# Attention weights as a product of two exponentials and the adjacency, in a graph kernel with eight slots per loop body

## The chip, the cores and the metric

The kernel runs on one core of a Trainium2 chip. The metric is the device time of one execution in microseconds, as a median of several runs. The core's engines run side by side and meet only at semaphores: TensorE (PE in the profile, its weight loads PEld), VectorE (DVE), ScalarE (ACT), GpSimd (POOL) and SyncE (SP, which here only issues DMAs).

## The reference, cut to what matters

There are 64 graphs of 128 nodes with 128 features each; `adj` is a weighted adjacency matrix per graph. Two layers follow each other, each added to its input and normalised over the features.

```python
# layer 0, for each graph
hi = x @ W1[:H]; hj = x @ W1[H:]
h = relu(hi[:, None, :] + hj[None, :, :] + b1)      # 128 x 128 pairs of nodes, 128 features
y = layernorm(h @ W2 + b2) * gamma + beta
x = layernorm(x + einsum('ij,ijh->ih', adj, y))
# layer 1, for each graph
Wh = x @ W_w.T + W_b
si = Wh @ a_w[:C]; sj = Wh @ a_w[C:]
e = exp(si[:, None] + sj[None, :] + a_b) * adj
x = layernorm(x + (e / sum(e, axis=1)) @ x)
```

Nearly all arithmetic is in layer 0: 64 x 16384 pairs, each times a 128 x 128 matrix. The change lies in the two lines of layer 1 with `exp` and with the division by the row sum.

## The kernel before

A slot is one pass of the schedule over one graph. In slot t, four graphs are in work at different stages: the pair product of graph t ("pairs"), the preparation of graph t+1 ("prep": transposes of x and adj, products with W1), the weighted sum over the pairs of graph t-1 ("gather"), and all the rest of graph t-2 ("tail": back to the feature basis, first layernorm, attention, second layernorm, output). There are 66 slots, 0 to 65. The first 6 and the last 4 are written out; the 56 between are 7 turns of a loop whose body holds 8 slots.

A slot has 16 units. In each unit:

- GpSimd adds hi and hj for a block of 1024 columns (L259), four units ahead, in a ring of four buffers; it waits until TensorE has read the old block.
- ScalarE applies relu in place (L288), two units ahead, and then copies two quarters of the product, y, from PSUM to SBUF (L270). A quarter is one PSUM bank of four 128x128 tiles. Quarters are numbered through the slot, so unit u has quarters 2u and 2u+1.
- TensorE multiplies the relu's output by w_pair (L529), four 128x128 tiles into each of four rotating PSUM banks. Before a quarter it waits until VectorE has done with the quarter four before (q_done).
- VectorE multiplies y in PSUM by its copy in SBUF and sums along the row, one tile at a time (L515), four tiles a quarter, for the variance of the pair layernorm. It waits for the copy of each quarter.

Every TensorE product of 128x128 goes through `mm` (L529): four matmuls on the four groups of 32 columns of the array. In the trace each of these matmuls is two instructions (the data are float32), so one mm call shows as 8 matmul instructions. The weighted sums (L574, 8 instructions of 512 columns) follow the pair product in units 4, 6, 7, 9, 10, 12, 13 and 15.

Between these, in an order written out by hand by unit (u) and, on VectorE, by quarter of a unit (e), stand the small steps of the tail. VectorE has four such places e in each unit, and after each place it does two tiles of squares. The steps around the change, all on graph t-2:

- Unit 7: VectorE normalises into x1e (L469; x1e has a 129th column of ones, for the row sum), then forms the scores si (L472) and sj (L475), each one column.
- Unit 8: ScalarE spreads si over 128 columns, si_cols (L346).
- Unit 10: TensorE transposes si_cols into PSUM (L596); ScalarE takes exp with sj as bias (L351), which gives exp(s_i + s_j) with j on the partitions; VectorE multiplies by adjS, the adjacency transposed, into eT (L485).
- Unit 12: TensorE multiplies eT with x1e (L600): the weighted sum over the neighbours, and in column 128 the row sum. VectorE takes the reciprocal of the row sum (L488), scales and adds x1e (L492), and begins the statistics of the second layernorm (L496, L501).
- Unit 14: ScalarE forms the reciprocal root (L355, L357), VectorE writes x_out (L507), and SyncE stores it.

Two other steps stand near: in unit 9 TensorE makes the W1 products of the next graph and VectorE copies them out in `project`, at (9, 0); in unit 5 GpSimd copies adjT to adjS, behind a wait for the last reader of the old adjS.

Of the kernel before, what the change touches and what calls it, by code (L numbers as in the profile page):

```python
# [33 lines left out]
def gnn_pair_kernel(nc, x, adj, W1, b1, W2, b2, gamma, beta, Ww, Wb, aw, ab, out):  # L34
    F32 = mybir.dt.float32
    ALU = mybir.AluOpType
    ACT = mybir.ActivationFunctionType

    B, S, H = x.shape
# [23 lines left out]
    with ctx:  # L63
# [6 lines left out]
        def sem(name):  # L70
# [26 lines left out]
        sj, si, si_cols, s_terms = sb("sj", [S, 1]), sb("si", [S, 1]), sb("si_cols", [S, S]), sb("s_terms", [S, 2, K])  # L97
# [16 lines left out]
        eT = sb("eT", [S, S])  # L114
# [10 lines left out]
        x1p = ex = att_ps[:, 2 * K:3 * K]  # L125
# [17 lines left out]
        x1_ready, score_ps_s = sem("x1_ready"), sem("scores_in_psum")  # L143
        ex_ready, eT_ready, att_done = sem("exp_ready"), sem("eT_ready"), sem("attention_in_psum")
        rz_ready, x2p_ready, st2_ready, mv2_ready, ln2_ready, rs2_ready = sem("rz_ready"), sem("x2p_ready"), sem("st2_ready"), sem("mv2_ready"), sem("ln2_ready"), sem("rs2_ready")
        adj_sum_ready, beta_part_ready, x_beta_ready, sj_ready, si_ready, si_cols_ready = (
            sem(n) for n in ("adj_sum_ready", "beta_part_ready", "x_beta_ready", "sj_ready", "si_ready", "si_cols_ready"))
# [57 lines left out]
        def _(pool):  # L205
# [11 lines left out]
            def pair_weights(t, p, early):  # L217
# [8 lines left out]
                if early >= 3:  # L226

                    pool.wait_ge(eT_ready, t - 2)
# [39 lines left out]
        def _(act):  # L268
# [37 lines left out]
            def slot(t, half, p, pairs, prep, gather, tail, early):  # L306
                for u in range(UNITS):
# [36 lines left out]
                    if tail and u == 8:  # L344
                        act.wait_ge(si_ready, t - 1)
                        nc.scalar.activation(si_cols[:], ones[:], ACT.Identity, scale=si[:, 0:1]).then_inc(si_cols_ready, 1)  # L346
                    if tail and u == 10:
                        act.wait_ge(score_ps_s, t - 1)

                        act.wait_ge(sj_ready, t - 1)  # L350
                        nc.scalar.activation(ex, tail_ps[:, 3, :], ACT.Exp, bias=sj[:, 0:1]).then_inc(ex_ready, 1)  # L351
# [23 lines left out]
        def _(dve):  # L375
# [49 lines left out]
            def slot(t, half, p, pairs, prep, gather, tail, early):  # L425

                for u, e in ((u, e) for u in range(UNITS) for e in range(2 * QPU)):
# [43 lines left out]
                    if tail and (u, e) == (7, 1):  # L471
                        nc.vector.tensor_tensor_reduce(out=s_terms[:, 1, :], in0=x1p, in1=v1row[:], scale=rs1[:, 0:1], scalar=0.0,  # L472
                                                       op0=ALU.mult, op1=ALU.add, accum_out=si[:, 0:1]).then_inc(si_ready, 1)
                    if tail and (u, e) == (7, 2):
                        nc.vector.tensor_tensor_reduce(out=s_terms[:, 0, :], in0=x1p, in1=v2row[:], scale=rs1[:, 0:1], scalar=score_c[:, 0:1],  # L475
                                                       op0=ALU.mult, op1=ALU.add, accum_out=sj[:, 0:1]).then_inc(sj_ready, 1)
# [5 lines left out]
                    if tail and (u, e) == (10, 0):  # L482
                        dve.wait_ge(ex_ready, t - 1)
                        dve.wait_ge(adjS_ready, t - 1)
                        nc.vector.tensor_tensor(eT[:], ex, adjS[:, p, :], ALU.mult).then_inc(eT_ready, 1)  # L485
                    if tail and (u, e) == (12, 0):
                        dve.wait_ge(att_done, t - 1)
                        nc.vector.reciprocal(rz[:], att_ps[:, K:K + 1]).then_inc(rz_ready, 1)  # L488
                    if tail and (u, e) == (12, 1):
# [4 lines left out]
                    if tail and (u, e) == (12, 2):  # L494
                        dve.wait_ge(x2p_ready, t - 1)
                        nc.vector.bn_stats(st2[:], x2p).then_inc(st2_ready, 1)  # L496
                    if tail and (u, e) == (12, 3):
# [27 lines left out]
        def _(pe):  # L525
# [52 lines left out]
            def slot(t, half, p, pairs, prep, gather, tail, early):  # L578
                for u in range(UNITS):
# [13 lines left out]
                    if tail and u == 10:  # L593

                        pe.wait_ge(si_cols_ready, t - 1)
                        mm(tail_ps[:, 3, :], si_cols[:], ident[:]).then_inc(score_ps_s, 1)  # L596
                    if tail and u == 12:
                        pe.wait_ge(eT_ready, t - 1)
                        pe.wait_ge(x1_ready, t - 1)
                        mm(att_ps[:, 0:K + 1], eT[:], x1e[:]).then_inc(att_done, 1)  # L600
# [44 lines left out]
```

## Time and profile before

| | |
|---|---|
| median of 3 runs | 2457.67 us (2455.99 to 2457.86) |
| the profiled execution | 2456.72 us |
| its span, first to last instruction | 2454.9 us |
| granted TensorE clock, mean | 0.994 of full speed |
| busy, share of the span: TensorE matmul | 2390.1 us, 97% |
| ScalarE | 2231.9 us, 91% |
| VectorE | 2117.0 us, 86% |
| GpSimd | 2022.4 us, 82% |
| DMA read and written over the span | 9 GB/s |

The busy times of an engine's instructions overlap in the trace, and on TensorE strongly: a matmul's record is longer than its distance to the next. The page's chain of waits follows the work that ended last back from the last instruction; its shares are PE 83%, ACT 9%, "issue" 4%, DVE 3%. "issue" is time in which the engine waited for nothing that the profile shows.

### The profile page before, as it was taken

What the parts mean: (1) busy time and instruction counts of PE and PEld (TensorE: products, weight loads), DVE (VectorE), ACT (ScalarE), POOL (GpSimd) and SP (SyncE); (2) the same over time, 40 slices, a digit from 0 to 9 for tenths busy, and PEclk for the clock granted to TensorE, in tenths of its full rate; (3) what the DMA queues carried; (4) which work ended last, traced back from release to release, by engine and by line L of the source; (5) the groups of instructions that cost most, each with busy time, mean ns of one, the idle gap of its engine ahead of it and who ended that gap; (6) DMA issues with size and microseconds to landing.
All of it is one profiled execution on the core that took longest, in us unless ns stands there. A gap on an engine that the chain in (4) does not pass through costs nothing.

```text
span 2454.9 us, 181527 instructions
## 1 busy us (share of the span) xinstructions
PE 2390.1 (97%) x73792; PEld 2063.3 (84%) x73792; DVE 2117.0 (86%) x17817; ACT 2231.9 (91%) x3841; POOL 2022.4 (82%) x1227
## 2 busy tenths in 40 slices
PE   8999999999999999999999999999999999999997
PEld 7888888878888888888888878888888888888885
DVE  7888888888888888888888888888888888888887
ACT  7999999989999899998999989999899998999996
POOL 7888888878888788888888878888788887888884
PEclk9999999999999999999999999999999999999999
DMA  0000000000000000000000000000000000000000
GB/s 20 11 13 15 11 15 16 10 17 12 14 16 10 17 16 10 16 13 14 15 10 15 15 12 15 10 15 16 11 16 11 14 15 11 15 16 10 15 11 8
DMA packets 48687, 33.45 MB, mean 14 GB/s; under 512 B 6208, under 2 KB 47808, under 8 KB 47808
## 3 DMA queue, kind: packets, MB, share of 16 engines
q1 hardware_dynamic: 46512, 21.12, 3.1%
q8 instruction: 601, 9.85, 1.7%
q14 instruction: 278, 2.28, 0.3%
q10 hardware_dynamic: 1296, 0.20, 0.0%
HBM read 17.11 MB, written 4.19 MB: 9 GB/s over the span
## 4 chain that ended last, share of the span: by engine, by line
PE 83%; ACT 9%; issue 4%; DVE 3%; POOL 0%; ACTq 0%; DMA 0%; DVEq 0%
PE y_ps L529 61%; PE agg_ps L574 18%; ACT h L288 5%; ACT y L270 3%; PE prep_ps L529 2%; DVE squares L515 2%; PE tail_ps L529 1%; ACT beta_part L328 1%; ACT ln_v L317 1%; PE att_ps L529 1%; DVE q L515 0%; POOL h L259 0%; ACT rstd L322 0%; DMA beta_rows<-in_L_gnn_beta_dram 0%; ACTq L367 0%
## 5 line engine op out<-in xcount | busy, mean ns | idle before, releaser
L259 POOL TENSOR_TENSOR h<-bT,aT 128x1024 f32<-128x1024 f32 x1024 | 1950.2, 1916 | 376.0 <-PE y_ps L529 354.8
L529 PEld LDWEIGHTS y_ps<-w_pair,h 128*32 128x32 f32 x65536 | 1837.8, 110 | 289.8 <-issue 208.2
L515 DVE CUSTOM_DVE_ANT_0 squares<-y_ps,y 128x128 bf16<-128x128 f32 x8192 | 1849.1, 286 | 265.9 <-ACT y L270 257.6
L529 PE MATMUL y_ps<-w_pair,h 128*32 128x128 f32 x65536 | 1973.3, 274 | 42.8 <-issue 25.3
L270 ACT ACTIVATE y<-y_ps 128x508 f32<-128x508 f32 x2048 | 1163.5, 596 | 164.7 <-PE y_ps L529 159.5
L288 ACT ACTIVATE h<-h 128x1024 f32<-128x1024 f32 x1024 | 1084.8, 1059 | 26.6 <-issue 14.9
L515 DVE DVE_READ_ACCUMULATOR2_ANT q<- 128x1 f32 x8192 | 679.6, 83 | 0.0
L574 PE MATMUL agg_ps<-y,wz 128*32 128x512 f32 x4096 | 548.7, 594 | 0.0
L574 PEld LDWEIGHTS agg_ps<-y,wz 128*32 128x32 f32 x4096 | 137.3, 110 | 3.8 <-issue 3.8
L451 DVE SCALAR_TENSOR_TENSOR o_sb<-agg_ps,part,o_sb 128x128 f32<-128x128 f32 x192 | 66.5, 346 | 0.2
L233 POOL TENSOR_TENSOR wz<-adjT,rstd 128x128 f32<-128x128 f32 x64 | 33.5, 523 | 34.2 <-ACT rstd L322 34.2
L529 PEld LDWEIGHTS tail_ps<-ident,si_cols 128*32 128x32 f32 x512 | 19.9, 110 | 37.6 <-issue 32.7
L507 DVE TENSOR_SCALAR x_out<-att_ps,mv,rs 128x128 f32<-128x128 f32 x64 | 26.2, 410 | 28.2 <-ACT rs L357 28.2
L529 PEld LDWEIGHTS tail_ps<-w_back,oT_sb 128*32 128x32 f32 x512 | 18.9, 110 | 36.0 <-issue 33.8
L245 POOL TENSOR_TENSOR x_beta<-beta_part,x_res 128x128 f32<-128x128 f32 x64 | 29.4, 459 | 11.7 <-ACT beta_part L328 11.5
L433 DVE TENSOR_SCALAR tail_ps<-q,bnorm 128x128 f32<-128x128 f32 x64 | 22.7, 354 | 15.3 <-issue 13.2
L469 DVE TENSOR_SCALAR x1e<-att_ps,mv,rs 128x128 f32<-128x128 f32 x64 | 26.2, 410 | 7.0 <-ACT rs L340 3.1
L529 PE MATMUL tail_ps<-ident,si_cols 128*32 128x128 f32 x512 | 27.9, 275 | 3.2 <-ACT si_cols L346 3.2
L529 PE MATMUL tail_ps<-ident,o_sb 128*32 128x128 f32 x512 | 26.0, 274 | 4.9 <-DVE o_sb L451 4.2
L529 PE MATMUL prep_ps<-ident,x_in 128*32 128x128 f32 x512 | 27.2, 275 | 3.1 <-DMA x_in<-in_x_dram 3.1
L529 PE MATMUL att_ps<-x1e,eT 128*32 128x129 f32 x512 | 28.1, 276 | 0.8 <-DVE eT L485 0.8
L328 ACT ACTIVATE beta_part<-beta_rows,adj_sum 128x128 f32<-128x128 f32 x64 | 25.4, 397 | 3.4 <-DVE adj_sum L439 3.4
(90 smaller groups left out, 725.2 us busy)
## 6 DMA issues: line engine op xcount, KB each, us to landing
x_in<-in_x_dram SPq DMA_DIRECT2D x64, 64.0 KB, 2.3
adj_in<-in_adj_dram SPq DMA_DIRECT2D x64, 64.0 KB, 2.5
x_res<-in_x_dram SPq DMA_DIRECT2D x64, 64.0 KB, 2.0
adj_res<-in_adj_dram SPq DMA_DIRECT2D x64, 64.0 KB, 2.4
out_dram<-x_out SPq DMA_DIRECT2D x64, 64.0 KB, 1.6
w<-in_L_gnn_W_dram ACTq DMA_DIRECT2D x1, 64.0 KB, 2.3
w1a<-in_L_gnn_W_dram SPq DMA_DIRECT2D x1, 64.0 KB, 2.2
w1b<-in_L_gnn_W_dram SPq DMA_DIRECT2D x1, 64.0 KB, 2.2
```

The costliest lines, as they stand in the source:

```text
L233: nc.gpsimd.tensor_tensor(columns, adjT[:, 1 - p, :].rearrange("j (g c s) -> j g c s", g=GROUPS, s=CHUNK), rstd[:].rearrange("j (c s g) -> ...
L245: nc.gpsimd.tensor_tensor(x_beta[:], beta_part[:], x_res[:, p, :], ALU.add).then_inc(x_beta_ready, 1)
L259: nc.gpsimd.tensor_tensor(h[:, u % HRING].rearrange("k (r g) s -> k r g s", g=GROUPS), bT[:, p, :].unsqueeze(1).unsqueeze(1).broadcast_to( ...
L270: return nc.scalar.activation(dst, src, ACT.Copy)
L288: nc.scalar.activation(h[:, u % HRING], h[:, u % HRING], ACT.Relu).then_inc(h_ready, 1)
L328: nc.scalar.activation(beta_part[:], beta_rows[:], ACT.Identity, scale=adj_sum[:, 0:1]).then_inc(beta_part_ready, 1)
L451: nc.vector.scalar_tensor_tensor(out=o_sb[:], in0=agg_ps[:, e * K:(e + 1) * K], scalar=part[:, e:e + 1], in1=o_sb[:], op0=ALU.mult, op1=AL ...
L469: nc.vector.tensor_scalar(x1e[:, 0:K], x1p, mv1[:, 0:1], rs1[:, 0:1], ALU.subtract, ALU.mult).then_inc(x1_ready, 1)
L507: nc.vector.tensor_scalar(x_out[:], x2p, mv2[:, 0:1], rs2[:, 0:1], ALU.subtract, ALU.mult).then_inc(out_ready, 1)
L515: last = nc.vector.tensor_tensor_reduce(out=squares[:, k % YRING, n, :], in0=y_ps[k % YRING][:, n, :], in1=y[:, p, i, :], scale=1.0, scala ...
L529: last = nc.tensor.matmul(dst[cols], lhsT[:, cols], rhs, start=True, stop=True, tile_position=(0, g * GROUP))
L574: last = nc.tensor.matmul(agg_ps[g * GROUP:(g + 1) * GROUP, :], wz[:, g, chunk, :], y_chunk[:, :, g, :], start=(chunk == 0), stop=(chunk = ...
```

## The change

The exponential of the sum is written as a product: exp(s_i + s_j + a) = exp(s_i) exp(s_j + a). The factor of row j goes onto row j of x1e, and the factor of row i onto the results.

- In place of si_cols, its transpose, the 128x128 exp and the product eT, ScalarE takes exp of the two columns s_i and s_j + a in unit 9 (e_ij) and then scales x1e, ones included, by exp(s_j + a) into x1s (128x129).
- TensorE multiplies adjS, as it is, with x1s, in unit 11 in place of unit 12. The product of unit 10 is gone.
- Column 128 of the result is now the row sum without exp(s_i). VectorE multiplies it by exp(s_i) (z_e), takes the reciprocal (z_r), and multiplies by exp(s_i) again (rz), at the places (11, 0) to (11, 2). Then follow the residual step at (11, 3), and the statistics at (12, 0) and (12, 1).
- GpSimd's wait before it writes adjS is now for att_done, since the attention product is the last reader.

```diff
@@ tiles
-        sj, si, si_cols, s_terms = sb("sj", [S, 1]), sb("si", [S, 1]), sb("si_cols", [S, S]), sb("s_terms", [S, 2, K])
+        s_ij, e_ij, s_terms = sb("s_ij", [S, 2]), sb("e_ij", [S, 2]), sb("s_terms", [S, 2, K])
+        x1s = sb("x1s", [S, K + 1])
-        eT = sb("eT", [S, S])
-        x1p = ex = att_ps[:, 2 * K:3 * K]
+        x1p = att_ps[:, 2 * K:3 * K]
+        z_e, z_r = att_ps[:, K + 1:K + 2], att_ps[:, K + 2:K + 3]
@@ GpSimd
-                    pool.wait_ge(eT_ready, t - 2)
+                    pool.wait_ge(att_done, t - 2)
@@ ScalarE
-                    if tail and u == 8:
+                    if tail and u == 9:
                         act.wait_ge(si_ready, t - 1)
-                        nc.scalar.activation(si_cols[:], ones[:], ACT.Identity, scale=si[:, 0:1]).then_inc(si_cols_ready, 1)
-                    if tail and u == 10:
-                        act.wait_ge(score_ps_s, t - 1)
-
                         act.wait_ge(sj_ready, t - 1)
-                        nc.scalar.activation(ex, tail_ps[:, 3, :], ACT.Exp, bias=sj[:, 0:1]).then_inc(ex_ready, 1)
+                        if early >= 3:
+
+                            act.wait_ge(rz_ready, t - 2)
+                        nc.scalar.activation(e_ij[:], s_ij[:], ACT.Exp).then_inc(e_ready, 1)
+                        act.wait_ge(e_ready, t - 1)
+                        act.wait_ge(x1_ready, t - 1)
+                        nc.scalar.activation(x1s[:], x1e[:], ACT.Identity, scale=e_ij[:, 1:2]).then_inc(x1s_ready, 1)
@@ VectorE
-                    if tail and (u, e) == (10, 0):
-                        dve.wait_ge(ex_ready, t - 1)
-                        dve.wait_ge(adjS_ready, t - 1)
-                        nc.vector.tensor_tensor(eT[:], ex, adjS[:, p, :], ALU.mult).then_inc(eT_ready, 1)
-                    if tail and (u, e) == (12, 0):
+                    if tail and (u, e) == (11, 0):
                         dve.wait_ge(att_done, t - 1)
-                        nc.vector.reciprocal(rz[:], att_ps[:, K:K + 1]).then_inc(rz_ready, 1)
-                    if tail and (u, e) == (12, 1):
+                        dve.wait_ge(e_ready, t - 1)
+                        nc.vector.tensor_scalar(z_e, att_ps[:, K:K + 1], e_ij[:, 0:1], None, ALU.mult).then_inc(z_e_ready, 1)
+                    if tail and (u, e) == (11, 1):
+                        dve.wait_ge(z_e_ready, t - 1)
+                        nc.vector.reciprocal(z_r, z_e).then_inc(z_r_ready, 1)
+                    if tail and (u, e) == (11, 2):
+                        dve.wait_ge(z_r_ready, t - 1)
+                        nc.vector.tensor_scalar(rz[:], z_r, e_ij[:, 0:1], None, ALU.mult).then_inc(rz_ready, 1)
+                    if tail and (u, e) == (11, 3):
                         dve.wait_ge(rz_ready, t - 1)
                         dve.wait_ge(x1_ready, t - 1)
                         nc.vector.scalar_tensor_tensor(out=x2p, in0=att_ps[:, 0:K], scalar=rz[:, 0:1], in1=x1e[:, 0:K],
                                                        op0=ALU.mult, op1=ALU.add).then_inc(x2p_ready, 1)
-                    if tail and (u, e) == (12, 2):
+                    if tail and (u, e) == (12, 0):
                         dve.wait_ge(x2p_ready, t - 1)
                         nc.vector.bn_stats(st2[:], x2p).then_inc(st2_ready, 1)
-                    if tail and (u, e) == (12, 3):
+                    if tail and (u, e) == (12, 1):
                         dve.wait_ge(st2_ready, t - 1)
@@ TensorE
-                    if tail and u == 10:
-
-                        pe.wait_ge(si_cols_ready, t - 1)
-                        mm(tail_ps[:, 3, :], si_cols[:], ident[:]).then_inc(score_ps_s, 1)
-                    if tail and u == 12:
-                        pe.wait_ge(eT_ready, t - 1)
-                        pe.wait_ge(x1_ready, t - 1)
-                        mm(att_ps[:, 0:K + 1], eT[:], x1e[:]).then_inc(att_done, 1)
+                    if tail and u == 11:
+                        pe.wait_ge(x1s_ready, t - 1)
+                        pe.wait_ge(adjS_ready, t - 1)
+                        mm(att_ps[:, 0:K + 1], adjS[:, p, :], x1s[:]).then_inc(att_done, 1)
```

## Rows read from the trace of the kernel before

**Rows 1.** Chain of waits, one slot: start us, us, engine, output, line, instructions.

```profile
1241.62 1.75 PE y_ps L529 x64
...
1243.36 0.86 PE agg_ps L574 x8
1244.22 0.22 PE tail_ps L529 x8
```

**Rows 2.** Instructions by line, whole run: count | busy us, mean ns | idle before.

```profile
L529 PE MATMUL tail_ps<-ident,si_cols 128*32 128x128 f32 x512 | 27.9, 275 | 3.2 <-ACT si_cols L346 3.2
```

**Rows 3.** Timeline of TensorE, restarts in unit 4: start us, us, work [idle before <-releaser].

```profile
1229.01 1.96 PE L529 MATMUL y_ps<-w_pair,h 128*32 128x128 f32 x64 [0.16 <-DVE q L515]
...
1266.23 1.95 PE L529 MATMUL y_ps<-w_pair,h 128*32 128x128 f32 x64 [0.16 <-DVE q L515]
```

**Rows 4.** Busy us by engine, one slot: PE, PEld, DVE, ACT, POOL, PEclk, DMA.

```profile
1229.01:1266.23 37.22, 36.98 (x1153) 31.62 (x1153) 32.91 (x279) 34.81 (x61) 31.59 (x20) 1.00 0.05 14
```

**Rows 5.** Timeline of ScalarE, unit 0 of a slot.

```profile
1223.17 0.60 ACT L270 ACTIVATE y<-y_ps 128x508 f32<-128x508 f32 x1 [0.28 <-PE y_ps L529]
```

**Rows 6.** Timeline of TensorE around two turns of the loop.

```profile
504.36 1.96 PE L529 MATMUL y_ps<-w_pair,h 128*32 128x128 f32 x64 [0.17 <-DVE q L515]
...
537.76 2.15 PE L529 MATMUL y_ps<-w_pair,h 128*32 128x128 f32 x66 [3.83 <-issue]
...
584.98 1.96 PE L529 MATMUL y_ps<-w_pair,h 128*32 128x128 f32 x64 [0.16 <-DVE q L515]
...
1112.91 1.95 PE L529 MATMUL y_ps<-w_pair,h 128*32 128x128 f32 x64 [0.16 <-DVE q L515]
...
1191.79 1.95 PE L529 MATMUL y_ps<-w_pair,h 128*32 128x128 f32 x64 [0.17 <-DVE q L515]
```

**Rows 7.** Instructions by line, whole run: the small operations of ScalarE and VectorE.

```profile
L346 ACT ACTIVATE si_cols<-ones,si 128x128 f32<-128x128 f32 x64 | 26.8, 419 | 1.5 <-DVE si L472 1.5
...
L351 ACT ACTIVATE att_ps<-tail_ps,sj 128x128 f32<-128x128 f32 x64 | 21.3, 333 | 2.3 <-PE tail_ps L529 2.3
...
L485 DVE TENSOR_TENSOR eT<-att_ps,adjS 128x128 f32<-128x128 f32 x64 | 18.6, 291 | 4.3 <-ACT att_ps L351 3.4
...
L357 ACT ACTIVATE rs<-ln 128x1 f32<-128x1 f32 x64 | 13.0, 203 | 2.0
...
L488 DVE RECIPROCAL rz<-att_ps 128x1 f32<-128x1 f32 x64 | 10.4, 163 | 1.3 <-PE att_ps L529 1.3
```

**Rows 8.** Timeline of ScalarE: relu of unit 11, a copy of unit 9, relu of unit 12.

```profile
1204.52 1.05 ACT L288 ACTIVATE h<-h 128x1024 f32<-128x1024 f32 x1
1205.47 0.59 ACT L270 ACTIVATE y<-y_ps 128x508 f32<-128x508 f32 x1
...
1206.70 1.06 ACT L288 ACTIVATE h<-h 128x1024 f32<-128x1024 f32 x1
```

**Rows 9.** Timeline of VectorE: first squares of quarter 18, the pause before quarter 22.

```profile
1206.29 0.28 DVE L515 CUSTOM_DVE_ANT_0 squares<-y_ps,y 128x128 bf16<-128x128 f32 x1
...
1210.51 0.08 DVE L515 DVE_READ_ACCUMULATOR2_ANT q<- 128x1 f32 x1
1211.39 0.29 DVE L515 CUSTOM_DVE_ANT_0 squares<-y_ps,y 128x128 bf16<-128x128 f32 x1 [0.80 <-ACT y L270]
```

**Rows 10.** Timeline of TensorE: the pair product of unit 11.

```profile
1209.64 1.93 PE L529 MATMUL y_ps<-w_pair,h 128*32 128x128 f32 x64
```

**Rows 11.** Timeline of all engines, slot 65: the attention when it stands alone.

```profile
2448.01 0.40 ACT L346 ACTIVATE si_cols<-ones,si 128x128 f32<-128x128 f32 x1 [0.74 <-DVE si L472]
2448.23 0.08 DVE L475 DVE_READ_ACCUMULATOR2_ANT sj<- 128x1 f32 x1
...
2448.47 0.65 PE L529 MATMUL tail_ps<-ident,si_cols 128*32 128x128 f32 x8 [3.24 <-ACT si_cols L346]
...
2449.91 0.66 PE L529 MATMUL att_ps<-x1e,eT 128*32 128x129 f32 x8 [0.79 <-DVE eT L485]
2450.63 0.17 DVE L488 RECIPROCAL rz<-att_ps 128x1 f32<-128x1 f32 x1 [0.78 <-PE att_ps L529]
```

More of the change, by code:

```diff
@@ L142, in gnn_pair_kernel @@
         x1p_ready, st1_ready, mv1_ready, ln1_ready, rs1_ready = sem("x1p_ready"), sem("st1_ready"), sem("mv1_ready"), sem("ln1_ready"), sem("rs1_ready")
-        x1_ready, score_ps_s = sem("x1_ready"), sem("scores_in_psum")
-        ex_ready, eT_ready, att_done = sem("exp_ready"), sem("eT_ready"), sem("attention_in_psum")
+        x1_ready, e_ready, x1s_ready, att_done = sem("x1_ready"), sem("exp_ready"), sem("x1s_ready"), sem("attention_in_psum")
+        z_e_ready, z_r_ready = sem("row_sum_scaled"), sem("row_sum_inverted")
         rz_ready, x2p_ready, st2_ready, mv2_ready, ln2_ready, rs2_ready = sem("rz_ready"), sem("x2p_ready"), sem("st2_ready"), sem("mv2_ready"), sem("ln2_ready"), sem("rs2_ready")
-        adj_sum_ready, beta_part_ready, x_beta_ready, sj_ready, si_ready, si_cols_ready = (
-            sem(n) for n in ("adj_sum_ready", "beta_part_ready", "x_beta_ready", "sj_ready", "si_ready", "si_cols_ready"))
+        adj_sum_ready, beta_part_ready, x_beta_ready, sj_ready, si_ready = (
+            sem(n) for n in ("adj_sum_ready", "beta_part_ready", "x_beta_ready", "sj_ready", "si_ready"))
         s_passed = sem("statistics_wait_passed")
@@ L472, in slot @@
                         nc.vector.tensor_tensor_reduce(out=s_terms[:, 1, :], in0=x1p, in1=v1row[:], scale=rs1[:, 0:1], scalar=0.0,
-                                                       op0=ALU.mult, op1=ALU.add, accum_out=si[:, 0:1]).then_inc(si_ready, 1)
+                                                       op0=ALU.mult, op1=ALU.add, accum_out=s_ij[:, 0:1]).then_inc(si_ready, 1)
                     if tail and (u, e) == (7, 2):
                         nc.vector.tensor_tensor_reduce(out=s_terms[:, 0, :], in0=x1p, in1=v2row[:], scale=rs1[:, 0:1], scalar=score_c[:, 0:1],
-                                                       op0=ALU.mult, op1=ALU.add, accum_out=sj[:, 0:1]).then_inc(sj_ready, 1)
+                                                       op0=ALU.mult, op1=ALU.add, accum_out=s_ij[:, 1:2]).then_inc(sj_ready, 1)
                     if prep and (u, e) == (9, 0):
```

## The prediction

> **What bounds the kernel now.** I read the chain of waits first, then one slot of it (a slot is one graph of the batch, 16 units), then the engines' busy time in that slot, and last the places where TensorE stops. In the chain nearly every piece between two slot starts is TensorE: 64 matmul instructions of the pair product take 1.75 us, 8 of a weighted sum 0.86 us, and each small product (one call of mm, 8 instructions in the trace) 0.22 us, the score product of L596 among them [rows 1]. One matmul record of the score product lasts 275 ns [rows 2], yet 8 of them pass in 0.22 us: records of the engine overlap, so I count by distances between starts, not by record lengths. By those, a slot holds 16 x 1.745 = 27.92 us of pair product, 8 x 0.857 = 6.86 us of weighted sums and 8 small products x 0.218 = 1.75 us: 36.53 us. TensorE resumes at the same place of two successive slots at 1229.01 and 1266.23 [rows 3], so a slot lasts 37.22 us. The 0.69 us left over is one bubble at the slot's start. The granted clock in the slot is 1.00, the full 2.4 GHz level, and the other engines are busy 32.9 (VectorE), 34.8 (ScalarE) and 31.6 us (GpSimd) of the 37.22 [rows 4]. ScalarE is the closest second, with 2.4 us to spare.
>
> The bubble has its own chain: at 1223.17 ScalarE's copy of a y tile starts after 0.28 us of idling for TensorE [rows 5], and from there relus and copies on ScalarE and the squares on VectorE run to 1229.01, where TensorE resumes after a wait for VectorE [rows 3]. Its head hangs on TensorE's work of the slot before. What is taken off TensorE in units 1 to 15 moves that head earlier and leaves the length of the bubble as it is, as long as the copy still waits for TensorE there.
>
> Besides, each turn of the loop body costs time: from 504.36 to 584.98 are two slots, 80.62 us, with a 3.83 us stop of TensorE whose releaser is "issue" [rows 6]. That is 6.18 us above 2 x 37.22. The shortest of the six turns, between 1112.91 and 1191.79, gives 78.88 - 74.44 = 4.44 us; the other four lie between.
>
> **The change, part by part.**
>
> *TensorE loses one product of the two in the score path.* In unit 10 the transposing product of si_cols (8 instructions) goes. The attention product stays with the same shape (128 rows by 129 columns), now from adjS and x1s, and moves from unit 12 to unit 11. Price by the chain: 0.218 us, on the path [rows 1]. It is on the path in slots 2 to 63: 62 x 0.218 = 13.5 us. In slot 64 there are only sums and tail products; its product also lies in a row of TensorE work: 0.2 us more. A lower bound is nothing (if another engine sets the slot, see the rivals).
>
> A rule stands against this price. The Trainium skill, "TensorE: Matmul & The Clock Gate", section "Back-to-back issue gap", gives an isolated gap of N/2.4 + 2.5 ns, 56 ns for N = 128; 8 of them would be 0.45 us and the removal would be worth 28 us. The trace does not agree: 64 instructions of that width take 1.75 us, 27 ns each; here four of them work on four column groups side by side.
>
> *ScalarE.* Out go the broadcast of si in unit 8 (0.419 us) and the 128x128 exp in unit 10 (0.333 us). In come, both in unit 9 between a relu and the y copies, an exp of 128x2 and the scaling of x1e (128x129). Nearest rows: the exp of one column, 0.203 us, and the broadcast, 0.419 us with a pointer scale, 129 columns being 1% more [rows 7]. The exp can hardly be under 0.15 us or over 0.42. Sum: 0.62 in for 0.75 out, ScalarE is relieved by 0.13 us in each slot; that is not on the path and counts as nothing. What counts is that the work is now in one piece. The x1s scaling waits on ScalarE's own exp, and behind it are queued the copies of quarters 18 and 19. By starts, the pair takes about 0.25 + 0.40 = 0.65 us, so quarter 18's copy starts at about 1206.1 instead of 1205.47 [rows 8]. Who waits: VectorE's squares of quarter 18, which start at 1206.29 today [rows 9], right after the projection that keeps VectorE busy anyway; they move by about 0.45 us and end at about 1207.7. TensorE needs them only for quarter 22, whose product starts at 1209.64 [rows 10] and about 1209.4 after the change. The cover is 1.7 us, and by unit 10, where the exp is gone, ScalarE has its delay back. The relu of unit 12, behind those copies, then starts at about 1207.1 in place of 1206.70, with its reader at 1211.4. So the cost is nothing; without the cover it would be 0.65 us in each slot. The wait for sj, written in unit 7, is over in unit 9, and the one on rz_ready looks at a slot that has ended.
>
> *TensorE's wait in unit 11* is for x1s, ready at about 1206.6, when TensorE comes by at 1209.4: 2.8 us of slack. Nothing hangs on adjS_ready either, whose copy GpSimd makes in unit 5.
>
> *VectorE.* Out goes the 128x128 product eT in unit 10 (0.291 us). In come two operations on one column, z_e and rz, beside the reciprocal that was there (0.163 us [rows 7]). I take 0.16 us each; the ends are nothing, if they vanish in the overlap of neighbours, and 0.29, a whole 128x128 operation. Net +0.03 us. They are spread one by one through unit 11 between pairs of squares, and each waits for the one before, which has two squares of 0.21 us behind it, so their own waits are over on arrival. The first waits for att_done with all squares of unit 11 queued behind it. VectorE sits idle there for 0.80 us today, waiting for quarter 22 [rows 9]; its last read of quarter 21 starts at 1210.51, or 1210.3 after the change. att_done comes about 0.7 us after 1209.4 (0.72 is what the product takes when it stands alone [rows 11]), so it is there first. Unit 11 becomes longer on VectorE by 0.16 + 0.16 + 0.16 + 0.35 = 0.83 us (with the residual step, which moves up from unit 12), unit 12 shorter by 0.52; TensorE wants quarter 22's squares for unit 13, over 1.5 us later. Cost nothing. The second statistics come earlier, so the norm of unit 14 waits for nothing new.
>
> *GpSimd and SyncE.* One wait changes its semaphore (att_done of the slot before instead of eT_ready), long over in unit 5. No DMA is added or moved.
>
> *The end, slot 65, is serial.* Today the reciprocal begins at 2450.63, 2.62 us after the start of si_cols at 2448.01 [rows 11]. After: sj is read out by 2448.31 and seen at 2448.35. Then the exp, 0.23 with its hand-over, the scaling, 0.46 (2448.01 to 2448.47), and the product, 0.72 (2449.91 to 2450.63), so VectorE begins at 2449.76, 0.87 earlier; two one-column operations more, 0.20 each with their hand-over, take 0.40 back. Gain 0.47 us; between 0.2 and 0.9 with the prices above.
>
> **Sum.** 13.5 + 0.2 + 0.5 = 14.2 us. The profiled execution took 2456.72 us with a span of 2454.9; 2456.72 - 14.2 = 2442.5. The median of the runs is 2457.67, 0.95 above it: 2443.5 us, or -0.58%.
>
> **Rivals.**
> (a) *Another engine sets the slot.* If ScalarE's rate decided the whole slot, TensorE's 0.218 us would only widen the bubble. The gain is then the end alone, 0.5 us: 2457 us. Against it: ScalarE waits for TensorE at 1223.17 [rows 5] and has 2.4 us of slack in a slot, eleven times what is removed. 7%.
> (b) *The piece of ScalarE work in unit 9 reaches TensorE.* It decides from the point where the squares of quarter 18 end later than TensorE asks for quarter 22, 1.7 us from today. Price 0.65 - 0.22 = 0.43 us in each of 62 slots: +27 us, 2484 us. The same would follow if att_done kept VectorE in unit 11. Against: both covers are two to three times the delay. 3%.
> (c) *The loop turns shift.* The body is shorter by 128 of 18,448 TensorE instructions (8 x 1153 matmuls [rows 4] and as many weight loads), and a turn's cost moved between 4.4 and 6.2 us within one run; the six make 33.4 us. All at the low end is -7 us, all at the high end +4: 2436.5 to 2447.5 us. This is no case of its own but the range's width.
> (d) *The removal is worth more than by distance.* If the product cost TensorE a queue delay of its own as well, or the page's gap held, 62 x 0.45 us = 28 us: 2429 us. 3%.
> (e) Partial: the gain arrives in most slots only by half, 2450 us. For it: nothing that I found; 6%.
>
> **How the numbers follow.** Forecast case 81%, (e) 6%, (a) 7%, (b) 3%, (d) 3%. The likeliest time is 2443.5. The range takes the turns' bounds and reaches to the half gain: 2436.5 to 2450.5 us; outside are (a), (b), (d) and a tail of the main case, about 15%. What a measurement can tell from no change is 0.2%, 4.9 us, so "same" is 2452.8 to 2462.6. Faster 0.89, same 0.07, slower 0.04.
>
> **What would show it.** Right: TensorE's restart at the same place of successive slots 37.00 us apart in place of 37.22; the small products in the chain seven in number; the bubble still about 0.7 us; the new exp and scaling at 0.20 and 0.42 us; no new TensorE wait in units 10 to 13; ScalarE's first copy of unit 9 about 0.6 us later against TensorE. Wrong: slots still 37.22 (a); a stop of TensorE for VectorE's squares in units 11 or 12, or for x1s (b); turns outside 4.4 to 6.2 us (c).

## The result, and the profile after

The changed kernel takes 2437.91 us (median of 4 runs, 2434.96 to 2439.61) against 2456.83 us for the kernel before on the same chip: a ratio of 0.9922, 95% interval 0.9906 to 0.9937, 18.9 us less. The forecast was 2443.5 us, 14.2 us less, with a range of 2436.5 to 2450.5. The profiled execution took 2439.17 us; its span is 17.5 us shorter than the one before, 2454.9 us. The 18.9 us are a difference of medians; what follows counts in the two profiled executions.

The page of the changed kernel, its span and TensorE's row:

```profile
span 2437.4 us, 180631 instructions
...
PE 2377.7 (98%) x73280; PEld 2049.3 (84%) x73280; DVE 2119.3 (87%) x17881; ACT 2221.6 (91%) x3841; POOL 2021.5 (83%) x1227
```

TensorE has 512 matmul instructions fewer, 8 in each of 64 tail slots. VectorE has become slightly busier, ScalarE 10 us less busy. The timeline of TensorE in unit 4 of two successive slots, which answers to [rows 3], and the busy time of each engine (TensorE, its loads, VectorE, ScalarE, GpSimd) in one slot, which answers to [rows 4]:

```profile
1367.43 1.95 PE L535 MATMUL y_ps<-w_pair,h 128*32 128x128 f32 x64 [0.17 <-DVE q L521]
...
1404.43 1.95 PE L535 MATMUL y_ps<-w_pair,h 128*32 128x128 f32 x64 [0.17 <-DVE q L521]
```

```profile
691.73:728.73 37.00, 36.76 (x1144) 31.39 (x1145) 33.06 (x280) 34.59 (x61) 31.53 (x20) 1.00 0.05 14
```

A slot now lasts 37.00 us, exactly the 0.22 us less that the missing product takes. TensorE's busy time fell by the same 0.22 (36.98 to 36.76), so its idle time in the slot, 0.24 us, has not changed. The chain of waits through that slot, which answers to [rows 1]; seven small products are left in it:

```profile
706.94 1.75 PE y_ps L535 x64
708.69 0.86 PE agg_ps L580 x8
709.54 0.22 PE att_ps L535 x8
709.76 3.49 PE y_ps L535 x128
...
722.89 0.04 ACT y L271
```

The chain again leaves TensorE at a y copy in the next slot's unit 0 (722.89) and comes back at 728.73, 5.84 us later; before it was 1223.17 to 1229.01, also 5.84. The bubble is untouched.

The slots give 0.22 x 61 = 13.4 us between the restart in slot 1 and that in slot 63. The whole stretch became shorter by 16.2 us (55.45 to 2401.25 before, 55.29 to 2384.87 after), so there is a second gain of about 3 us that is no slot's. It lies at the returns of the loop. The timeline of TensorE over the first return, which answers to [rows 6]:

```profile
502.29 1.96 PE L535 MATMUL y_ps<-w_pair,h 128*32 128x128 f32 x64 [0.17 <-DVE q L521]
...
534.39 5.72 PE L535 MATMUL y_ps<-w_pair,h 128*32 128x128 f32 x189 [2.75 <-issue]
...
579.61 1.95 PE L535 MATMUL y_ps<-w_pair,h 128*32 128x128 f32 x64 [0.17 <-DVE q L521]
```

This return costs 579.61 - 502.29 - 2 x 37.00 = 3.32 us, where the kernel before paid 6.18. After the first stop TensorE runs through 189 matmuls. In the kernel before it stops a second time, 66 matmuls on:

```profile
541.10 3.69 PE L529 MATMUL y_ps<-w_pair,h 128*32 128x128 f32 x126 [1.20 <-issue]
```

For all six returns, and for what the seven bodies hold above their slots, I took the same differences between restarts:

| | slot | six returns | seven bodies | together |
|---|---|---|---|---|
| before | 37.22 | 33.4 | 2.6 | 36.1 |
| changed | 37.00 | 23.8 | 9.2 | 32.9 |

So the returns are 9.6 us cheaper, and the bodies hold 6.6 us more of short stops ("issue", 0.2 to 0.7 us). Both sums stood at no change in the forecast's own sum; its range allowed the returns 7 us less, and the bodies nothing. The end of the program brings about 1.1 us (from the restart in slot 63 to the last instruction 52.5 for 53.7 us), the start 0.2.

### The profile page after: what moved, and what is told of

It reads as the page before. It is cut to its first block, busy times and chain, and to the rows that moved or that the text cites. A ratio compares the mean times of both kernels' runs of the same rounds, so it can differ in the third digit from the quotient of the medians.

```text
span 2437.4 us, 180631 instructions
## 1 busy us (share of the span) xinstructions
PE 2377.7 (98%) x73280; PEld 2049.3 (84%) x73280; DVE 2119.3 (87%) x17881; ACT 2221.6 (91%) x3841; POOL 2021.5 (83%) x1227
## 4 chain that ended last, share of the span: by engine, by line
PE 80%; ACT 10%; issue 5%; DVE 3%; POOL 2%; ACTq 0%; DMA 0%; POOLq 0%; DVEq 0%
PE y_ps L535 59%; PE agg_ps L580 17%; ACT h L289 5%; ACT y L271 3%; PE prep_ps L535 2%; DVE squares L521 2%; POOL h L260 2%; ACT beta_part L329 1%; PE tail_ps L535 1%; ACT ln_v L318 1%; PE att_ps L535 1%; DVE q L521 0%; ACT rstd L323 0%; ACTq L370 0%; DMA beta_rows<-in_L_gnn_beta_dram 0%
## 5 line engine op out<-in xcount | busy, mean ns | idle before, releaser
L289 ACT ACTIVATE h<-h 128x1024 f32<-128x1024 f32 x1024 | 1085.0, 1060 | 23.8 <-POOL h L260 20.5
L535 PEld LDWEIGHTS att_ps<-x1s,adjS 128*32 128x32 f32 x512 | 20.2, 110 | 37.6 <-issue 32.7
L535 PEld LDWEIGHTS tail_ps<-w_back,oT_sb 128*32 128x32 f32 x512 | 18.2, 111 | 37.2 <-issue 36.1
L535 PE MATMUL att_ps<-x1s,adjS 128*32 128x129 f32 x512 | 28.1, 275 | 3.5 <-ACT x1s L354 3.5
L535 PE MATMUL prep_ps<-xT,w1b 128*32 128x128 f32 x512 | 28.0, 275 | 0.0
```

The costliest lines, as they stand in the source:

```text
L289: nc.scalar.activation(h[:, u % HRING], h[:, u % HRING], ACT.Relu).then_inc(h_ready, 1)
L535: last = nc.tensor.matmul(dst[cols], lhsT[:, cols], rhs, start=True, stop=True, tile_position=(0, g * GROUP))
```

## The experiments

All times are medians, beside runs of the kernel before on the same chip: 2457.84 us in the first group of four, 2457.96 in the second, 2456.38 in the third.

### The product put back

```diff
                         pe.wait_ge(adjS_ready, t - 1)
+                        mm(att_ps[:, 0:K], adjS[:, p, :], ident[:])
                         mm(att_ps[:, 0:K + 1], adjS[:, p, :], x1s[:]).then_inc(att_done, 1)
```

> The changed kernel with one more 128-column product of TensorE per tail slot, right before the attention product and overwritten by it (its inputs are adjS and the identity). Theory A (the changed kernel gained 0.22 us a slot because one product went): slots are 37.22 us again instead of 37.00, and the time rises by 62 x 0.218 = 13.5 us over the changed kernel. Rival B (the gain came from the lighter ScalarE and VectorE work, or from the operations moved): slots stay at 37.00. On the rest of the gain, some 4.7 us of the medians: if it hangs on the length of the loop body's code, six turns cost about 33 us again and the time is that of the kernel before, 2457; if it hangs on something else, 2451.

Measured: 2457.29 us, ratio to before 0.9998 (0.9988 to 1.0007). The timeline of TensorE in two successive slots:

```profile
1038.20 1.96 PE L535 MATMUL y_ps<-w_pair,h 128*32 128x128 f32 x64 [0.17 <-DVE q L521]
...
1075.43 1.96 PE L535 MATMUL y_ps<-w_pair,h 128*32 128x128 f32 x64 [0.17 <-DVE q L521]
```

The slot is 37.23 us, and the whole gain is gone, the part beyond the slots with it: its returns and bodies sum to 37.4 us (34.0 in the returns). All that the change did on ScalarE and VectorE together is worth nothing that the slots show (37.23 for 37.22), and in the time no more than the interval leaves, some 2 us. Theory A holds, rival B falls. The product cost 0.22 us and not the 0.45 us that the rule in the Trainium skill, "TensorE: Matmul & The Clock Gate", section "Back-to-back issue gap", would give; rival (d) falls as well.

### The same product taken out of the kernel before

```diff
-                        pe.wait_ge(si_cols_ready, t - 1)
-                        mm(tail_ps[:, 3, :], si_cols[:], ident[:]).then_inc(score_ps_s, 1)
...
-                        act.wait_ge(score_ps_s, t - 1)
+                        act.wait_ge(si_cols_ready, t - 1)
...
-                        nc.scalar.activation(ex, tail_ps[:, 3, :], ACT.Exp, bias=sj[:, 0:1]).then_inc(ex_ready, 1)
+                        nc.scalar.activation(ex, si_cols[:], ACT.Exp, bias=sj[:, 0:1]).then_inc(ex_ready, 1)
```

> The kernel before without the transposing product of unit 10; the exp reads si_cols as it is in SBUF, so the weights are wrong and the attention's result with them, and every other operation stands. Theory A (the whole gain, the part beyond the slots too, hangs on this one product): slots 37.00 us, loop returns near the changed kernel's 4.0 us, time 2438. Rival C (the product gives 13.7 us, and the other 5 come from ScalarE's and VectorE's shorter code or work): slots 37.00, returns still 5.6 us, time 2443.

Here the scores are not transposed, so the attention weights are not the right ones; the exp has the same shape and reads SBUF in place of PSUM. Measured: 2438.04 us, ratio 0.9922 (0.9905 to 0.9938), the changed kernel's to the last digit. Slots are 37.01 us (767.44 to 804.45), the returns sum to 24.7 us and the bodies' stops to 7.8. Everything else of the kernel before is in place, the two large ScalarE operations and eT too. One product of TensorE in each slot is the whole change in time, from both sides, within intervals of some 2 us (put back) and 4 us (taken out); rival C falls.

### Fewer returns

```diff
-    PEEL, LOOP_END, BODY = 6, B - 2, 8
+    PEEL, LOOP_END, BODY = 6, B - 2, 14
```

> The changed kernel with 14 slots per loop body: 4 turns of the body instead of 7, so three returns to the body's start instead of six. Theory T (each return costs 3.2 to 4.7 us, because all engines then wait for instructions): slots 37.00 us as before, the time falls by 3 x 4.0 = 12 us to about 2426. Rival V (the cost hangs on the volume of code that is read, which stays the same): no change, 2438.

> The kernel before with 14 slots per loop body. Theory T: three returns fewer at 5.6 us each, about -17 us, 2440. Rival V: 2457. If returns cost the two kernels differently for a reason that lies in the kernels and not in the position of their code, the distance between this and the changed kernel with 14 slots is 14.0 us from the slots plus three returns' difference, 5 us; if it lies in the position of the code, the difference may have either sign.

Measured: 2426.40 us for the changed kernel (ratio to before, with 8 slots, 0.9867, 0.9851 to 0.9884), 2438.26 us for the kernel before (0.9917, 0.9901 to 0.9934). Theory T holds for both. Three returns are left in each: 3.89, 4.66 and 4.70 us in the changed kernel, 4.08, 4.29 and 4.46 in the kernel before, 13.3 and 12.8 us. With this body length the returns cost both the same. The code of the loop starts where it starts with 8 slots; what differs from there is how long the body is and where it ends. The distance between the kernels is 11.9 us here and 18.9 with 8 slots, so dearer returns are no property of the kernel before itself, for which 19 us were expected here too: the 13.6 us of 62 slots are the change's own, the 5 us beyond them are not.

The same with 28 slots, one return:

> The changed kernel with 28 slots per loop body: two turns, one return. Theory T: 5 x 4.0 = 20 us less than with 8 slots, about 2418. Rival V: 2438. A third way: longer code costs stops inside the body, as the 0.9 to 2.1 us that the bodies of the changed kernel hold above 37.00 a slot; then it comes out between.

and with all 56, none:

> The changed kernel with all 56 slots in one body: no return at all. If a return costs its 4 to 5 us and longer code nothing, 2415.6 - 4.9 = 2411; if reading straight code has stops of its own, as the 0.3 to 0.4 us stops once or twice in eight slots suggest, those stay (about 1 us in eight slots) and the time is the same 2411; if a long program costs more than that, above 2416.

Measured: 2415.62 us (ratio 0.9825, 0.9808 to 0.9841) and 2415.26 us (0.9832, 0.9815 to 0.9848). With 28 the expectation of 2418 was close. The one return, in the timeline of TensorE:

```profile
1206.80 1.95 PE L535 MATMUL y_ps<-w_pair,h 128*32 128x128 f32 x64 [0.16 <-DVE q L521]
...
1276.25 7.12 PE L535 MATMUL y_ps<-w_pair,h 128*32 128x128 f32 x192 [3.11 <-ACT h L289]
...
1285.66 1.95 PE L535 MATMUL y_ps<-w_pair,h 128*32 128x128 f32 x64 [0.25 <-DVE q L521]
```

It costs 78.86 - 74.00 = 4.86 us; the last to hold TensorE there is ScalarE's relu, not its own code. The step to no return at all should have given these 4.9 us and gave 0.4. The timeline of the kernel with 56 slots in one body shows what came in its place:

```profile
1134.26 1.95 PE L535 MATMUL y_ps<-w_pair,h 128*32 128x128 f32 x64 [0.22 <-DVE q L521]
...
1171.35 1.96 PE L535 MATMUL y_ps<-w_pair,h 128*32 128x128 f32 x64 [0.22 <-DVE q L521]
```

A slot lasts 37.09 us there, 0.09 more than in the loops, with TensorE's wait for the squares at 0.22 in place of 0.17 us. Over 56 slots that is 5 us, all that the return cost. In the two profiled executions the kernel without a return is 2.8 us shorter (spans of 2414.2 and 2411.4 us), because its slots hold less of other delays; the medians do not show it. The first six slots, written out in all the kernels, have the same 37.08 us (131.31 - 94.01 = 37.30 in the kernel before, in place of 37.22). Why code written out runs slower by 0.09 us a slot, I did not settle. The version with 28 slots per body beats both kernels: 42 us under the kernel before, 22 under the changed one.

### The position of the code

The loop is untouched here; TensorE only gets products into its setup, where it waits for other engines.

```diff
+            for _ in range(4):
+                mm(tail_ps[:, 3, :], ident[:], ident[:])
             pe.wait_ge(s_w, 16 * 9)
             pe.wait_ge(s_setup_dve, 8)
```

> The changed kernel with 4 idle products (64 instructions of TensorE, loads counted) in the setup, where TensorE waits some 5 us anyway; the loop is the same, its code begins 64 instructions later. Position theory P (what a return costs depends on where the body's code starts in the blocks in which it is read): the six returns, 3.2 to 4.7 us now, change by 0.5 us or more each, and so does the sum of stops inside the bodies; the time moves by 3 us or more either way. Rival L (the length of the body sets it): returns and time as in the changed kernel, 2438.

> As the one before with 8 products, 128 instructions. P: another cost of the returns than with 0 and with 64. L: 2438 again.

> The kernel before with the same 8 idle products in its setup. The kernel before has 5.6 us a return. P: it moves, and if the changed kernel was only lucky in its position, some position brings this one near 4.0 us a return and 2448 us. L: 5.6 us a return and 2457.

Measured, with the sums of the returns and the stops in the bodies from the same differences as above:

| | median | ratio to before | six returns | seven bodies |
|---|---|---|---|---|
| changed | 2437.91 | 0.9922 | 23.8 | 9.2 |
| changed, 64 instructions later | 2438.74 | 0.9928 (0.9911 to 0.9944) | 27.1 | 4.4 |
| changed, 128 later | 2450.74 | 0.9974 (0.9964 to 0.9985) | 40.2 | 7.0 |
| before | 2456.83 | 1 | 33.4 | 2.6 |
| before, 128 later | 2473.21 | 1.0065 (1.0048 to 1.0082) | 51.1 | 2.8 |

Nothing in the loop differs between the changed kernel and its padded forms, and the restart in slot 1 comes no later with the padding (54.20 and 55.22 us beside 55.29), so the position of TensorE's code decides by itself over some 13 us, nearly as much as the change. Theory P holds in that the cost moves, and rival L, that length alone sets it, falls. With 64 instructions, though, the time did not move by the 3 us that P asked for: the returns rose by 3.3 us and the bodies fell by 4.8. That is hardly beyond what moves without any change of TensorE's code: the three kernels of the last two experiments below, which have the changed kernel's TensorE code, sum to 22.5, 24.5 and 26.3 us in the returns and 5.0, 4.1 and 5.0 in the bodies. And no padding tried brought the kernel before near the changed one's returns; 128 instructions made them dearer.

The timeline of TensorE's weight loads at the first return shows how. First the changed kernel, then 64 and 128 instructions later:

```profile
534.38 2.76 PEld L535 LDWEIGHTS y_ps<-w_pair,h 128*32 128x32 f32 x99 [3.66 <-issue]
537.40 2.44 PEld L535 LDWEIGHTS y_ps<-w_pair,h 128*32 128x32 f32 x90 [0.26 <-issue]
```

```profile
534.27 2.35 PEld L535 LDWEIGHTS y_ps<-w_pair,h 128*32 128x32 f32 x67 [3.51 <-issue]
537.29 4.14 PEld L535 LDWEIGHTS y_ps<-w_pair,h 128*32 128x32 f32 x122 [0.67 <-issue]
```

```profile
534.76 1.76 PEld L535 LDWEIGHTS y_ps<-w_pair,h 128*32 128x32 f32 x36 [3.61 <-issue]
538.32 5.86 PEld L535 LDWEIGHTS y_ps<-w_pair,h 128*32 128x32 f32 x154 [1.79 <-issue]
```

Next the kernel before, and it 128 instructions later:

```profile
537.75 1.88 PEld L529 LDWEIGHTS y_ps<-w_pair,h 128*32 128x32 f32 x67 [4.74 <-issue]
541.10 3.42 PEld L529 LDWEIGHTS y_ps<-w_pair,h 128*32 128x32 f32 x125 [1.47 <-issue]
```

```profile
535.72 0.15 PEld L529 LDWEIGHTS y_ps<-w_pair,h 128*32 128x32 f32 x4 [3.63 <-issue]
539.02 6.03 PEld L529 LDWEIGHTS y_ps<-w_pair,h 128*32 128x32 f32 x140 [3.15 <-issue]
```

After the return TensorE has 99, 67, 36, 67 and 4 loads, each with its matmul, before it must stop a second time. The padded code reaches that point some 32 loads and 32 matmuls earlier for each 64 instructions that it is shifted: the point lies at a fixed place of the code, while the loop's start is moved towards it. The kernel before fits into this row: its written-out slots 2 to 5 hold one product more each, 4 x 16 instructions with the loads, so its loop starts 64 instructions later than the changed kernel's, and it has the 67 loads of the changed kernel with 64 instructions of padding; with 128 more it has 4. The first to the second restart takes 3.0 to 3.6 us in all five (534.38 to 537.40, 537.75 to 541.10, 534.76 to 538.32). So what comes behind the point is there about 3 us after the first restart, and at 27 ns a pair 99 loads nearly fill that time (stop of the loads 0.26 us, of the matmuls none), 67 leave over a microsecond and 4 leave all of it. With 64 instructions of padding the 67 loads took 2.35 us and left 0.67, for the clock was low (below). Not each return shows the second stop: on the matmuls it is missing in two of six in the kernel before, and in five of six in the changed one. With 128 instructions of padding all six have it, 9.0 us together on the matmuls in the changed kernel and 16.8 in the kernel before.

A second cost follows from the stops. In some returns the granted clock falls from the 2.4 GHz level to the 1.2 GHz level about when TensorE resumes, after a stop of 2.3 to 3.9 us. Here are two stretches of the first return of the changed kernel with 128 instructions of padding, by engines; TensorE is busy through both. The column before the last two is the granted clock:

```profile
539.00:541.00 2.00, 2.00 (x44) 2.00 (x40) 0.09 (x1) 0.71 (x2) 0.67 (x1) 0.50 0.05 12
542.00:544.00 2.00, 2.00 (x84) 2.00 (x76) 1.36 (x12) 1.97 (x5) 1.58 (x4) 1.00 0.04 8
```

In 2 us it takes 40 weight loads at the low level and 76 at the high one. In windows of 1 us the low level lasts about 3.4 or 6.8 us each time. It comes at three of six returns in the changed kernel, at three in the kernel before (twice for 6.8 us), and at all six in both kernels with 128 instructions of padding, there for 6.8 us but for one. Where the clock stays high, a return costs some 0.6 us beyond its stops (3.32 for 2.75 us, the changed kernel's first); with 3.4 us at the low level it is 1.7 us (4.57 for 2.90, its fourth), with 6.8 us it is 2.3 to 2.7 us (5.81 for 3.47 in the kernel before, 7.15 for 2.77 and 1.82 with 128 instructions of padding in the changed one). So the 128 instructions cost twice, by the second stop and by the clock.

The removal of a product moved the loop's start 64 instructions away from that point, but this is only a part of why the returns became cheaper.

At the same start the changed kernel with 64 instructions of padding pays 27.1 us and the kernel before 33.4 (34.0 with the product put back into the changed one); most of the difference is in the first stops, 2.3 to 2.9 us in the one and 2.5 to 3.8 in the other (15.0 and 20.1 us together, 16.7 in the changed kernel). Their bodies differ by 128 instructions of TensorE, so their ends lie elsewhere. That the end has such a place too would fit, and so would the returns with 14 slots, and the first stops of the kernel before, whose sum fell from 20.1 to 15.6 us with 128 instructions of padding; but no run moved the end alone. Nor did any run explain the short stops in the bodies.

### ScalarE's piece of work in unit 9

```diff
+                        for n in range(2):
+                            nc.scalar.activation(spare[:, n, :], x1e[:], ACT.Identity, scale=e_ij[:, 1:2])
                         nc.scalar.activation(x1s[:], x1e[:], ACT.Identity, scale=e_ij[:, 1:2]).then_inc(x1s_ready, 1)
```

> The changed kernel with two more scalings of x1e (128x129, into tiles that nothing reads) ahead of the one in unit 9: about 0.8 us more of ScalarE in one piece in front of the y copies, in each slot. The prediction gave ScalarE's piece of work in unit 9 a cover of 1.7 us beyond what the change needs, and 2.4 us of slack in a slot. Cover theory: slots 37.00 us, time 2438. Rival (b) of the prediction (the piece is close to TensorE): slots longer by up to 0.8 us, up to 50 us.

> As the one before with five more scalings, 1.9 to 2.1 us of ScalarE. The cover of 1.7 us is used up: TensorE should show a stop before the pair products of unit 11, of 0.2 to 0.4 us, and the slot should be 37.2 to 37.4 us: 12 to 25 us more, 2450 to 2463. If ScalarE's slack over the whole slot is the limit rather than the local cover, it is less than 0.4 us a slot; if the cover is larger than worked out, nothing.

Measured: 2436.89 us (ratio 0.9915, 0.9898 to 0.9931) with two and 2437.08 us (0.9916, 0.9900 to 0.9933) with five more scalings; neither differs from the changed kernel. With two the expectation held; with five it was wrong by 12 us at least. One slot of the second by engines, then its timeline of ScalarE, VectorE and TensorE in units 9 to 11:

```profile
1028.29:1065.30 37.01, 36.76 (x1144) 31.40 (x1145) 32.78 (x280) 35.59 (x66) 31.54 (x20) 1.00 0.05 14
```

```profile
1042.20 1.57 ACT L355 ACTIVATE spare<-x1e,e_ij 128x129 f32<-128x129 f32 x5
1043.67 0.39 ACT L356 ACTIVATE x1s<-x1e,e_ij 128x129 f32<-128x129 f32 x1
1043.97 1.05 ACT L271 ACTIVATE y<-y_ps 128x508 f32<-128x508 f32 x2
```

```profile
1044.58 0.29 DVE L523 CUSTOM_DVE_ANT_0 squares<-y_ps,y 128x128 bf16<-128x128 f32 x1 [1.69 <-ACT y L271]
```

```profile
1045.93 0.40 PE L537 MATMUL att_ps<-x1s,adjS 128*32 128x129 f32 x8
1046.15 3.68 PE L537 MATMUL y_ps<-w_pair,h 128*32 128x128 f32 x128
```

The five scalings take 1.47 us from first start to the next operation's (1042.20 to 1043.67), 0.29 each, not the 0.39 of a record. The Trainium skill, "ScalarE: Activation LUTs", section "What ACT_TABLE_LOAD costs", says that activations in a row overlap by about 93 ns; the trace agrees, with 0.39 us for a record and 0.29 from start to start. VectorE waits 1.69 us for the late copy, its squares of quarter 18 end at about 1045.5, and TensorE asks for that bank at 1046.15. The cover that was put at 1.7 us is not used up: 0.65 us is left.

### VectorE's three small steps as one

```diff
-                        nc.vector.tensor_scalar(z_e, att_ps[:, K:K + 1], e_ij[:, 0:1], None, ALU.mult).then_inc(z_e_ready, 1)
...
-                        nc.vector.reciprocal(z_r, z_e).then_inc(z_r_ready, 1)
...
-                        nc.vector.tensor_scalar(rz[:], z_r, e_ij[:, 0:1], None, ALU.mult).then_inc(rz_ready, 1)
+                        nc.vector.reciprocal(rz[:], att_ps[:, K:K + 1]).then_inc(rz_ready, 1)
```

> The changed kernel without the two multiplications by exp(s_i) around the reciprocal: VectorE has one one-column operation where it had three (the attention result lacks the factor). Prediction's step: they cost nothing in the slots and 0.4 us in the last slot, so 2437.5. Rival: a chain of three dependent one-column steps, each behind a wait, holds VectorE and through it TensorE; then slots under 37.00.

Measured: 2433.69 us (2432.99 to 2440.17), ratio 0.9913 (0.9893 to 0.9933). The interval holds the changed kernel's 0.9922, so the time alone is inconclusive. The timeline of TensorE is not: slots are 37.00 us.

```profile
728.81 1.95 PE L529 MATMUL y_ps<-w_pair,h 128*32 128x128 f32 x64 [0.16 <-DVE q L515]
...
765.81 1.95 PE L529 MATMUL y_ps<-w_pair,h 128*32 128x128 f32 x64 [0.16 <-DVE q L515]
```

The two operations cost nothing in a slot; the rival falls. The span is 6.0 us shorter than the changed kernel's, of which 5.5 us are again returns and bodies (22.5 and 5.0 for 23.8 and 9.2), though TensorE's code is the same. The two kernels with more scalings, whose TensorE code is the same too, have 26.3 and 5.0 (two more) and 24.5 and 4.1 (five more). So the code of the other engines has a part in those stops, or they vary so much by themselves; one profile of each cannot say which. The low clock varies with them: it comes at one return with one reciprocal and with five more scalings, at three in the changed kernel, at six with two more.

## Why the prediction was right

*The bound.* TensorE sets the slot, the bubble hangs on it and keeps its length. Both were seen: 37.00 us and 5.84 us. The product's price, 0.218 us by the distances in the chain, was exact. Rival (a) falls with the first row of the result.

*ScalarE.* The timeline of ScalarE in the changed kernel's unit 9, which answers to [rows 8]:

```profile
705.40 0.19 ACT L351 ACTIVATE e_ij<-s_ij 128x2 f32<-128x2 f32 x1
705.63 0.40 ACT L354 ACTIVATE x1s<-x1e,e_ij 128x129 f32<-128x129 f32 x1
705.94 1.06 ACT L271 ACTIVATE y<-y_ps 128x508 f32<-128x508 f32 x2
```

0.19 and 0.40 us where 0.20 and 0.42 were taken, and 0.54 us from the exp's start to the copy's where 0.65 was. The relief is 0.22 us a slot (34.81 to 34.59) for the 0.13 worked out from records. The cover was argued rightly and mis-sized. In the changed kernel the squares of quarter 18 start at 706.55 and end about 0.9 us later, and TensorE asks for that bank at 709.58: 2.1 us, not 1.7. Half of the difference is the attention product, which now stands ahead of unit 11's pair product; the prediction let the pair product itself start at 1209.4. The five scalings then took 1.5 us of it, not the 2.0 that their records add up to.

*VectorE.* The timeline of VectorE in unit 11, which answers to [rows 9]:

```profile
710.23 0.22 DVE L488 TENSOR_SCALAR att_ps<-att_ps,e_ij 128x1 f32<-128x1 f32 x1
711.33 0.29 DVE L521 CUSTOM_DVE_ANT_0 squares<-y_ps,y 128x128 bf16<-128x128 f32 x1 [0.88 <-ACT y L271]
...
711.76 0.17 DVE L491 RECIPROCAL att_ps<-att_ps 128x1 f32<-128x1 f32 x1
...
712.25 0.21 DVE L494 TENSOR_SCALAR rz<-att_ps,e_ij 128x1 f32<-128x1 f32 x1
```

The first step falls into the pause before quarter 22, and 0.88 us of pause are still left behind it; att_done was there before VectorE came. The multiplications take 0.22 and 0.21 us, not the 0.16 of the reciprocal, which was taken as the nearest row: they read a second column as a scalar, the reciprocal does not, but no run shows that this is the reason. VectorE's slot is 0.15 us busier (33.06 for 32.91), not 0.03. It costs nothing, as said.

*The end.* The timeline of the last slot, which answers to [rows 11]:

```profile
2431.15 0.20 ACT L351 ACTIVATE e_ij<-s_ij 128x2 f32<-128x2 f32 x1 [1.13 <-DVE s_ij L478]
...
2431.84 0.66 PE L535 MATMUL att_ps<-x1s,adjS 128*32 128x129 f32 x8 [3.49 <-ACT x1s L354]
2432.57 0.23 DVE L488 TENSOR_SCALAR att_ps<-att_ps,e_ij 128x1 f32<-128x1 f32 x1 [1.50 <-PE att_ps L535]
...
2433.29 0.36 DVE L498 SCALAR_TENSOR_TENSOR att_ps<-att_ps,rz,x1e 128x128 f32<-128x128 f32 x1
```

From x1e's start to the residual step's it is 3.24 us (2430.05 to 2433.29) for 3.53 before (2447.30 to 2450.83): a gain of 0.3 us where 0.47 was forecast. The exp starts 0.17 us after the read of sj does, 0.05 later than assumed, and the three small steps take 0.72 us, not 0.60.

*The term that was mis-sized* is the one that stood in the sum at nothing: the returns of the loop. The prediction had it as "the range's width", from the spread within one run (4.4 to 6.2 us a return), and called values outside that span a sign that it was wrong. They were outside: four of six returns of the changed kernel are under 4.4 us. The spread of six returns of one program does not bound those of another program, whose code is shorter and lies elsewhere: the runs show from 22.5 to 51.1 us for six returns. The removed instructions, 64 ahead of the loop and 128 in its body, went with returns that are 9.6 us cheaper in the profiles, and the short stops in the bodies, which were not in the sum at all, took 6.6 us back. The 3 us that the two leave are most of what the profiled executions gained beyond the forecast (17.5 us for 14.2); the other 1.4 us lie between the profiled executions and the medians. That 2437.91 us fell into the range, 1.4 us above its lower end, is thus in part luck: the returns went past their bound, and a term that nobody had counted went the other way.

## What to carry to other kernels

Where one engine sets the pace through a whole period, a piece taken off it pays its distance between starts once a period, and nothing else in the period matters until a cover is used up; count delays by starts too, since records of ScalarE overlap as those of TensorE do. Keep apart what a change does in the period and what it does at the returns of an unrolled loop: the second can be as large as the first and turns on where the code happens to lie, so a padded form of the same kernel is the control for any gain under one per cent. Here a return costs what such a change gives in some twenty slots (4.0 to 5.6 us on average beside 0.22), and a longer body is worth more than the change.

## What the runs showed of the hardware

- A return of this loop costs 3.2 to 9.2 us. At the changed kernel's first one, all four compute engines are idle at once from 532.9 to 533.8 us. 64 or 128 instructions of TensorE ahead of the loop, in time that it idles anyway, left the median alone or raised it by 12.8 us (changed kernel), and 128 raised it by 15 us in the kernel before (2473.21 beside 2457.96).
- A return can have a second stop, at a fixed place of the code: what lies behind that place is there some 3 us after TensorE has resumed, and the fewer instructions lie between the loop's start and that place, the longer the stop, up to 2.9 us of the matmuls.
- After the stops of a return the granted clock of TensorE can fall to the 1.2 GHz level for 3.4 or 6.8 us (0.50 at 539 to 541 us with 128 instructions of padding, 40 loads in 2 us for 76): in 3 of 6 returns of the changed kernel, in 6 of 6 with that padding.
- Code written out in full runs a slot in 37.09 us where the loop takes 37.00, the same in the kernel before (37.30 for 37.22). Its cause is open.
